# A gated cross-attention and mixture-of-experts block: norms of two groups in one GpSimd series, an earlier slot table, and cuts moved between engines and units

## What is computed

```python
x = x + tanh(g_xattn) * xattn(layernorm(x), ctx, mask, W, b)     # softmax(relu(xW)relu(yW)^T) y
h = layernorm(x)
logits = h @ w_router                      # 8 experts
top_logits, top_idx = top_k(logits, 2)
scores = softmax(top_logits)
for e in range(8):                         # rows of expert e
    proj, gate = split(h_e @ fc1_w[e]);  out_e = silu(proj) * gate @ fc2_w[e]
moe = sum over the two experts of scores * out
shared = silu(h @ gate_w) * (h @ up_w) @ down_w
x = x + tanh(g_ffn) * (moe + shared)
```

## Time and profile before

| what | value |
| --- | --- |
| median of 3 runs | 241.2 us (240.91 to 241.91) |
| the profiled execution's own time | 239.41 us |
| its span, first to last instruction | 237.7 us |
| TensorE busy | 220.1 us (93%) |
| VectorE busy | 172.4 us (73%) |
| ScalarE busy | 130.0 us (55%) |
| GpSimd busy | 123.5 us (52%) |
| mean granted TensorE clock | 0.995 |

### The profile page before, as it was taken

The page is one execution under the profiler, slowest core; times in us unless marked ns, Lnnn a source line. Parts: engine busy times, 40 slices in busy tenths (PEclk is TensorE's granted clock), DMA queues, the critical chain, the costliest instruction groups (busy, mean ns, idle before and its releaser), DMA issues.

```text
span 237.7 us, 5259 instructions
## 1 busy us (share of the span) xinstructions
PE 220.1 (93%) x1413; PEld 192.5 (81%) x1413; DVE 172.4 (73%) x513; ACT 130.0 (55%) x316; POOL 123.5 (52%) x176
## 2 busy tenths in 40 slices
PE   7688999999899999889799999999999999999980
PEld 7588899978687888768688888888888888887860
DVE  1878897797568899996967656656656656655795
ACT  2565888772747644445226556556556556555320
POOL 1797796554868887888401334334334344344600
PEclk9999999999999999999999999999999999999997
DMA  5999940000132125322242433333333432108876
GB/s 148 295 397 407 398 163 3 0 0 25 45 110 74 67 92 201 124 81 92 68 121 60 134 115 93 108 114 93 99 119 89 117 97 68 49 26 296 271 270 265
DMA packets 18131, 32.05 MB, mean 135 GB/s; under 512 B 3046, under 2 KB 9323, under 8 KB 18104
## 3 DMA queue, kind: packets, MB, share of 16 engines
q1 hardware_dynamic: 14096, 22.28, 29.5%
q0 software_dynamic: 3408, 8.46, 9.6%
q10 hardware_dynamic: 600, 0.97, 1.3%
HBM read 19.95 MB, written 12.67 MB: 137 GB/s over the span
## 4 chain that ended last, share of the span: by engine, by line
PE 45%; POOL 8%; issue 6%; DVE 3%; DMA 2%; ACT 0%; SPq 0%; DVEq 0%; POOLq 0%
PE bank L977 38%; POOL rows L384 6%; PE bank L1221 4%; PE bank L1241 4%; POOL ew_lo L243 2%; DMA rows<-hrows,slot 1%; DVE acc L949 1%; DMA hrows<-rows 1%; DVE acc L698 1%; DVE act_lo L626 0%; SPq L280 0%; DVE act L912 0%; ACT act_hi L439 0%; ACT act L577 0%; DVEq L62 0%
## 5 line engine op out<-in xcount | busy, mean ns | idle before, releaser
L426 POOL DMA_INDIRECT parts<-y_out,dst x39 | 38.8, 995 | 71.1 <-DVE dst L906 67.5
L912 DVE TENSOR_TENSOR act<-act,bank 128x256 f32<-128x256 f32 x39 | 16.4, 421 | 34.4 <-ACT act L577 32.6
L384 POOL DMA_INDIRECT rows<-hrows,slot x32 | 34.2, 1069 | 12.3 <-issue 12.1
L577 ACT ACTIVATE act<-bank 128x256 f32<-128x256 f32 x39 | 15.0, 384 | 37.4 <-PE bank L977 37.4
L977 PE MATMUL bank<-ew_hi,m_xt_hi 128*128 x78 | 30.9, 396 | 0.1
L977 PE MATMUL bank<-ew_hi,m_xt_lo 128*128 x78 | 30.8, 395 | 0.0
L977 PE MATMUL bank<-ew_lo,m_xt_hi 128*128 x78 | 30.7, 394 | 0.0
L977 PE MATMUL bank<-ew_hi,act_hi 128*128 x78 | 25.2, 323 | 0.2 <-DVE act_lo L626 0.2
L439 ACT ACTIVATE act_hi<-act 128x512 fp32r<-128x512 f32 x16 | 10.1, 631 | 24.0 <-DVE act L685 24.0
L977 PE MATMUL bank<-ew_hi,act_lo 128*128 x78 | 21.9, 281 | 0.0
L977 PE MATMUL bank<-ew_lo,act_hi 128*128 x78 | 21.9, 281 | 0.0
(11 more groups left out here) (179 smaller groups left out, 653.1 us busy)
## 6 DMA issues: line engine op xcount, KB each, us to landing
ew_raw<-in_chunks SPq DMA_DIRECT2D x12, 512.0 KB, 10.7
hrows<-rows SPq DMA_DIRECT2D x39, 130.0 KB, 2.2
low_buf<-parts SPq DMA_DIRECT2D x4, 512.0 KB, 4.8
high_buf<-parts SPq DMA_DIRECT2D x4, 512.0 KB, 4.4
acc<-in_x SPq DMA_DIRECT2D x7, 256.0 KB, 4.8
sw_raw<-in_chunks SPq DMA_DIRECT2D x3, 512.0 KB, 8.5
out<-acc SPq DMA_DIRECT2D x3, 512.0 KB, 2.7
rows<-pad_rows SPq DMA_DIRECT2D x9, 130.0 KB
```

Of the source, the lines that this page charges most:

```text
L384: pool.indirect_dma_start(out=rows, out_offset=bass.IndirectOffsetOnAxis(ap=slot[:, h, k, i:i + 1], axis=0), in_=hrows[:, HT * h + i, :], ...
L426: pool.indirect_dma_start(out=parts, out_offset=bass.IndirectOffsetOnAxis(ap=dst[:, t:t + 1], axis=0), in_=y_out[:, t % SLOTS, :], in_offs ...
L577: a.activation(act[:, p, 0:I], M_H[p][:, 0:I], ACT.Silu).then_inc(s["m_sil"], 1)
L912: TT(act[:, p, 0:I], act[:, p, 0:I], M_H[p][:, I:2 * I], ALU.mult).then_inc(s["m_prod"], 1)
```

## The change

1. On GpSimd the norms of groups 6 and 7 are computed in one series over four columns (`rstd_second(NG - 2, 2)`) behind five scatters, in place of one series after the first and one after the third scatter.
2. `IN_A` goes from 7 to 8: chunk 7 is cut by GpSimd ahead of its first scatter, and ScalarE writes its high half between its steps `turn_h(NG - 4)` and `copy_eT(NG - 1)`. `MID` becomes four chunks (8, 10, 12, 14), `LAST` four (26 to 29). GpSimd cuts 16 low halves in place of 15, VectorE 14 in place of 15.
3. On VectorE `slots(0)` comes ahead of `residual(NG - 2)` and `turn_e(NG - 1)`.
4. The weight fields of the second half are written by VectorE, after `product_lo(4)`.
5. `LATER` is spread anew: units 7 and 8 have two cuts in place of one, unit 9 one in place of two, unit 12 one in place of three.
6. ScalarE's high cuts begin earlier (chunks 8 and 9 ahead of `silu(1)`, chunk 10 after `silu(2)`) and end with unit 11; its two last `norm_second` stand together.
7. TensorE: down of units 0 and 1 come ahead of `turn_h(NG - 2)`; gate and up of unit 3 stand between the last routers; `product(3)` on VectorE comes ahead of the logits of the second half, and `product_lo(3)` ahead of the second choice.
8. Fourteen matmuls in place of ten at the start, before there is work.

```diff
-IN_A = 7
+IN_A = 8
-MID = tuple(IN_A + 2 * i for i in range(5))
-LAST = tuple(range(CHUNKS - 3, CHUNKS))
-LATER = {3: 1, 4: 1, 5: 1, 6: 1, 7: 1, 8: 1, 9: 2, 10: 2, 11: 2, 12: 3}
+MID = tuple(IN_A + 2 * i for i in range(4))
+LAST = tuple(range(CHUNKS - 4, CHUNKS))
+LATER = {3: 1, 4: 1, 5: 1, 6: 1, 7: 2, 8: 2, 9: 1, 10: 2, 11: 2, 12: 1}
...
+            def rstd_second(g, m=1):
+                pool.wait_ge(s["mean2"], g + m)
+                sl = slice(GT * g, GT * (g + m))
...
+                    after(pool, "fields", 2)
+                    after(pool, "fields_last", 2 * h)
...
-            weight_fields(0)
-            scatter(0, 0, 1)
-            rstd_second(NG - 2)
-            scatter(0, 1, 3)
-            rstd_second(NG - 1)
-            scatter(0, 3, 8)
+            weight_fields_first()
+            scatter(0, 0, 5)
+            rstd_second(NG - 2, 2)
+            scatter(0, 5, 10)
             cut_lo(pool, MID[0])
-            scatter(0, 8, 12)
+            scatter(0, 10, 15)
             cut_lo(pool, MID[1])
-            scatter(0, 12, 2 * HT)
+            scatter(0, 15, 2 * HT)
+            scatter(1, 0, 5)
             cut_lo(pool, MID[2])
-            weight_fields(1)
-            scatter(1, 0, 6)
+            scatter(1, 5, 11)
             cut_lo(pool, MID[3])
-            scatter(1, 6, 11)
-            cut_lo(pool, MID[4])
             scatter(1, 11, 2 * HT)
...
-                if i == IN_A:
+                if i == SCH + 6:
                     after(a, "mt_ps", NG)
...
             turn_h(NG - 4)
+            cut_hi(IN_A - 1)
             copy_eT(NG - 1)
             weight_tanh(0)
             silu(0)
             turn_h(NG - 3)
-
-            norm_second(NG - 2)
+            for i in range(IN_A, IN_A + 2):
+                cut_hi(i)
             silu(1)
             silu_hi(0)
+            silu_hi(1)
+            silu(2)
+            cut_hi(IN_A + 2)
+
+            norm_second(NG - 2)
+            norm_second(NG - 1)
             turn_h(NG - 2)
-            silu_hi(1)
-
-            norm_second(NG - 1)
-            silu(2)
+            silu_hi(2)
             turn_h(NG - 1)
-            silu_hi(2)
-            i = IN_A
+            i = IN_A + 3
...
-                more = 3 if n < 6 else 2
+                more = 3 if n < 4 else 2 if n < 12 else 0
...
             weigh(0)
+            turn_h(NG - 4)
+            slots(0, bank[7])
             residual(NG - 2)
-            turn_h(NG - 4)
             turn_e(NG - 1)
-            slots(0, bank[7])
             turn_h(NG - 3)
...
+            product(3)
             read_logits(1)
             first_choice(1)
-            product(3)
+            product_lo(3)
             second_choice(1)
-            product_lo(3)
             cut_later(3)
...
             product_lo(4)
+            weight_fields_last()
             product(5)
...
-            for _ in range(10):
+            for _ in range(14):
...
             gate(2)
-            turn_h(NG - 2)
             up(2)
             after(pe, "resid", NT)
             after(pe, "placed", 1)
             down(0)
+            down(1)
+            turn_h(NG - 2)
+            gate(3)
             router(NG - 2)
             turn_h(NG - 1)
-            down(1)
+            up(3)
             router(NG - 1)
-            gate_up(3)
```

More of the change, by code:

```diff
@@ L198, in build @@
             xt_ps xt_h xt_l wt_h wt_l y_h y_l xp_ps xp sc_ps sc_in sc_max sc_exp eT_ps eT_h eT_l mt_ps s_inv resid stats2 mean2 pre2 pow2 rstd2 h_ready
-            hT_ps ht_h ht_l lg_ps lg_read rt picked rank_ps placed wts low_expert w_sign w_tanh fields slots t_expm scattered pads tb tiles_known
+            hT_ps ht_h ht_l lg_ps lg_read rt picked rank_ps placed wts low_expert w_sign w_tanh fields fields_last slots t_expm scattered pads tb tiles_known
             chunk_h chunk_lp chunk_lv gate_ps up_ps sil prod act_h act_l dn_ps dn_added
@@ L377, in scatter @@
                     after(pool, "h_ready", HT * (h + 1))
-                    after(pool, "fields", 2 * (h + 1))
+                    after(pool, "fields", 2)
+                    after(pool, "fields_last", 2 * h)
                     after(pool, "low_expert", h + 1)
@@ L828, in _, with weight_fields_last @@
             product(1)
-            turn_h(NG - 2)
             product_lo(1)
             product(2)
+            turn_h(NG - 2)
+            product_lo(2)
             turn_h(NG - 1)
-            product_lo(2)
+            def weight_fields_last():
+                sl = slice(HT, NT)
+                after(v, "w_tanh", NH)
+                TS(hrows[:, sl, D + 2], wsm[:, 3, sl], tgh[:, 0:1], tgh[:, 0:1], ALU.mult, ALU.add)\
+                    .then_inc(s["fields_last"], 1)
+                TS(hrows[:, sl, D + 3], wsm[:, 3, sl], tgh[:, 1:2], None, ALU.mult).then_inc(s["fields_last"], 1)
+            after(v, "tg_half", 2)
+            product(3)
             read_logits(1)
             first_choice(1)
-            product(3)
+            product_lo(3)
             second_choice(1)
-            product_lo(3)
             cut_later(3)
```

16 lines of the change are left out of this document (6 added, 10 removed).

## The result

The changed kernel takes 243.69 us (median of 5 runs, 242.58 to 244.05), the kernel before in the same sessions 241.45 us (median of 5, 240.91 to 241.96). The ratio is 1.0114, 95% interval [1.0071, 1.0156]: slower by 1.1%, where 239.8 us was forecast and 242.9 us was the upper end of the range. It is rival A, the burst on top of unit 10: the medians differ by 2.2 where A had 1.5. The profiled execution of after took 243.47 us with a span of 241.7, that of before 239.41 and 237.7.

What follows compares the result with a forecast made beforehand. It took GpSimd's scatter chain and VectorE's backlog, ahead of the first expert matmul, as the bound. +0.9 to product 5, -2.4 from there and 0.1 for the start made -1.4: 241.2 to 239.8 us, overall range 238.2 to 242.9.

Steps and rivals of the forecast that it cites:

- rival A: GpSimd's last four cuts catch unit 10's low half on VectorE; first expert matmul at 121.7, +1.5, 242.7 us; chance 0.28.
- what bounds it: Ahead of the expert part, GpSimd's scatter chain and, 1.4 us behind it, VectorE's backlog end last.
- a GpSimd cut stops VectorE's two-input work for its whole length: A GpSimd cut costs VectorE about 1.3 us between SBUF operands; a burst costs its whole length.
- The two collisions that were counted: GpSimd cuts at 89 and 98.4 fall on VectorE's work behind product 5, costing 2.5 us together.
- the head: Up to the slot table: chunk 7's cut holds the pick write, TensorE loses 1.1 us, first scatter stays at about 55.8.
- the four matmuls at the start: Four more TensorE matmuls at 0.46 end at about 8.0: 0 to 0.1 us lost, nothing to gain.
- the two waits for the normed rows: TensorE's waits of 0.50 and 0.62 us for groups 6 and 7 go, and smaller ones come.
- VectorE's load from product 5 to the low half of unit 8: VectorE's low half of unit 8 ends 19.6 us after 81.5, at 101.1; TensorE stands 1.6 for it.
- first term: Up to product 5, the end of unit 5: 81.5 for 80.6, so +0.9 us.
- second term: From product 5 to the first expert matmul: 37.2 us for 39.6, so -2.4.
- The step that failed: Unit 10's low half on VectorE, 106.6 to 107.3, is missed by GpSimd's burst from 107.0; 0.3 us decides.
- not let in at the seams: A VectorE instruction held by back-to-back GpSimd cuts waits until the last ends; one VectorE cut took 3.15 us.

Runs made afterwards that it cites:

- the small memsets: Even-table kernel with chunks 12 and 14 cut by VectorE in units 11 and 12, plus two one-column GpSimd memsets between late scatters: 238.45 us, ratio 0.994.
- the repeated order without late cuts: Even-table kernel with chunks 12 and 14 cut by VectorE in units 11 and 12, run again on another chip: 239.33 us, ratio 0.9909.
- both first edits: Changed kernel with chunk 7's GpSimd cut behind the norm series and the last four cuts held until unit 11's low half: 241.06 us, ratio 1.0037.
- two norm series: Kernel with both first edits, norms of groups 6 and 7 again in separate series after the first and third scatter: 240.36 us, ratio 1.0017.
- the last of the three kernels that stood still: Even-table kernel with two norm series and chunks 12 and 14 cut by VectorE in units 11 and 12: 253.56 us, ratio 1.0518.
- the filled gap: Changed kernel with seven extra 512-column matmuls on TensorE ahead of the wait in unit 10: 243.2 us, ratio 1.012.
- the spread alone: Changed kernel with only VectorE's cuts respread, one behind units 7 and 8, two behind 9 and 12: 243.29 us, median of 4 executions.

## Why the prediction was wrong

**Right: what bounds it.** That VectorE's backlog and the scatter chain end close together was confirmed on the kernel before (mending the one brought out the other). So was the premise that a GpSimd cut stops VectorE's two-input work for its whole length: 1.22 for a pick write, 1.53 for the slot product, 5.36 for the first of the two cuts of unit 10, and 0.69 for product 10, with one input in PSUM. The two collisions that were counted came, at 90.43 (on a cast, 1.57) and at 99.51 (on the cuts of unit 8, 2.86 for 1.41). The Trainium skill (GPSIMD Engine Reference, Key points) names two SBUF inputs or a two-port mode as the case for this contention; the rows agree, and add its length, and that a small cast with a single input is held too (1.60 in the earlier trace rows).

**Right: the head.** The pick write at 51.34 took 1.22 and the ranking began at 52.71 (predicted 52.9); the first scatter at 55.67 (55.8); the picks of the second half at 76.49 (76.1); unit 5 at 76.86 (76.2). The scatters end at 107.72 (107.0), and the four matmuls at the start cost nothing, as forecast: the next one is at 8.01 for 8.03. Of the two waits for the normed rows, which were to go, the 0.62 stayed: the series took 2.4 (62.5 to 64.9) for the 2.0 that I gave it. Its power took 1.27 on four columns, for 0.72 on two, so most of it goes by column.

**Right: VectorE's load from product 5 to the low half of unit 8.** 19.6 was the sum, 20.0 was measured (82.83 to 102.83), and the wait at unit 10's up half was 1.81 for 1.6.

**Wrong, first term: where product 5 begins.** 81.5 was predicted, 82.83 measured. 0.7 of it is unit 5's later start, of which the longer series can be 0.4. The other 0.7 is of a collision that I did not count: the GpSimd cut at 79.92 fell on the slot product at 79.86, which took 1.53 for 0.29. I counted two GpSimd cuts behind product 5 and none in the 5 us ahead of it, where by my own times (fifteen scatters, the series and a cut from 55.8 on) one had to stand at 78 to 80.

**Wrong, second term, and the one that decides: from product 5 to the first expert matmul.** It was put at 37.2 and is 41.4. The parts of these 4.2 are the slow up half of unit 10 (1.6), the wait at the up half of unit 12 (1.8), the longer waits in front of unit 10's halves (0.29 and 1.81 for 1.6, 0.5), and 0.3 in the last stretch (9.4 from the up half of unit 12, for 9.1).

**The step that failed** is the order of two events. I had the low half of unit 10 at 106.6 and the burst at 107.0, with 0.3 deciding, called the burst missing it the likeliest case, and gave the other 0.28. The burst came 0.7 late, in my favour. VectorE came 7.5 late: 1.3 from product 5, 1.6 from the clock, and the rest is the burst itself, since unit 10's cuts stood ahead of its low half and were now under it. A step that holds only if nothing in 25 us of VectorE's work slips by 0.3 should not have carried the forecast. GpSimd's chain could slip too, and did by 0.7, but VectorE's slips are larger and go mostly one way: each collision that wasn't counted puts it back by about 1.3. My argument against A, that three collisions must come true together, was the wrong way round, since the sum already had them in it.

**The size of A** was 242.7, and the measured medians are 243.69 against 241.45, +2.2 for its +1.5. That this is near is in part luck. In the profiles A had the first expert matmul at 121.7, and it was at 124.25: 1.3 of the 2.5 is product 5, 1.6 is the clock, the other small waits are 0.6, and the wait at unit 12 was 1.0 less than A had (1.78 for 2.8). The clock is a term that the prediction put at nothing. With the burst held back it still fell in the profile, and a ratio of 1.0037 was left; where the long wait was filled, it fell behind the next one.

**The test of the whole** is the version with the parts in another order. The same number of GpSimd and VectorE cuts, the same scatter chain, give ratios of 0.993 and 0.989, where the forecast was 0.994 (239.8 to 241.2). So the change's idea was sound, its order wasn't. How the gain divides is less sure, since each step is near the width of its interval. The first expert matmul, at 124.25 in after, is at 122.12 with the burst held back, at 120.46 and 119.91 with chunk 7 and then chunk 8 behind the norm series (1.6 of these 2.2 is the clock, which didn't fall), at 119.07 with the even table and at 118.68 without cuts between the late scatters. The ratios of these kernels are 1.0114, 1.0037, 1.0037, 1.0013, 0.993 and 0.9889. The edits were tried in this order alone. Of the rest of the change, the slot table ahead of the residual, the fields on VectorE, the earlier high cuts and TensorE's new order at the head were not tested by themselves.

## What to carry to other kernels

Where one engine can stop another for the length of an instruction, its queue is part of the other's schedule: put its bursts behind a semaphore of the victim, not behind whatever happens to come before them on its own queue. On the changed kernel that gave back 2 us, on the kernel before nothing, as TensorE then waited for something else. When a forecast rests on the order of two events a few tenths apart, ask in which direction each can slip and by how much; here one slipped by 0.7 and the other by nearly 3 before they met. And run an experiment's surprise a second time before explaining it: the largest effect of this study, 12 us, was not a property of the program's order.

## What the runs showed of the hardware that was not expected

**The clock after a wait.** Behind TensorE waits of 2.49, 2.51, 2.64, 3.23, 3.70 and 3.78 us the granted clock fell to its lower level, in each profile that has one. Behind eleven waits of 1.78 to 1.97, from 50 us on, it fell five times (after, the burst held back, chunk 7 first on the kernel before, the small memsets, the repeated order without late cuts) and six times not (both first edits, chunk 7 later, chunk 8 beside 7, two norm series, the second wait of after at 114.85, and one of 1.95 in the last of the three kernels that stood still). The price was 1.6 us in after. Which of the two happens was not settled. It can be a part of the scatter between executions: with the burst held back, the five with a mean granted clock of 0.984 to 0.988 took 241.4 to 242.6, and four of the five with 0.994 or 0.995 took 240.0 to 240.4.

**Who gets in at a seam.** A seam is the point between two GpSimd cuts back to back. The earlier trace rows showed one VectorE cut that was not let in there, and after has one that missed three seams. With the burst held back, VectorE's cut got in at a seam:

```profile
112.60 5.94 POOL L243 TENSOR_TENSOR ew_lo<-ew_raw,ew_hi 128x512 fp32r<-128x512 f32 x4 [5.18 <-DVE act_lo L628]
```

```profile
114.60 1.09 DVE L243 TENSOR_TENSOR ew_lo<-ew_raw,ew_hi 128x512 fp32r<-128x512 f32 x1
115.72 1.67 DVE L628 TENSOR_TENSOR act_lo<-act,act_hi 128x512 fp32r<-128x512 f32 x1
```

These are of the kernel with both first edits. VectorE lost 0.4 and 1.0 in place of 5, and GpSimd's four cuts took 5.94 in place of 5.04, so here the price was shared. The traces divide cleanly. Where the burst follows the last scatter (before, after, chunk 7 later, the filled gap, the spread alone) VectorE was never let in, and a burst of four took GpSimd 5.00 to 5.04. Where the burst waits for a semaphore, VectorE's cuts of unit 12 were let in, in each profile of the changed kernel's variants that has them inside the burst, and GpSimd's four took 5.92 to 6.46. What decides it is open: the semaphore ahead of the burst, or how long behind its start VectorE's cut comes, though in before it came 1.22 behind and was held, and in three of the others 1.24 behind and wasn't. So holding the burst back did two things, it moved the burst off unit 10 and it made it milder, and no run parts the two at unit 12. At unit 10 it is the move alone, as there the cuts took 1.41. The prediction's "not let in at the seams" held in after, and not in these.

**The power by column.** 0.72 on 128x2, 1.27 on 128x4, on GpSimd.

**Ten-microsecond stalls without a semaphore** in one loading of a program and not in the next, as told above.
